# Audio tower on one core: pair 0's norm statistics in two parts, fold copies on ScalarE, pair 0's class row as a matmul, and new queue positions

## What is computed

```
# tok: exponential moving average forward and backward over time, then a linear layer
ewma = (scan(x) + reverse_scan(x)) / 2                  # y[t] = 0.1 x[t] + 0.9 y[t-1]
h    = ewma @ W.T + b                                   # [16, 750, 256]
# attn: two selective scans over time on layernorm(h)
hidden = layernorm(h)
for l in 0, 1:
    delta = softplus(hidden @ Wd[l] + bd[l]);  u = hidden @ Wi[l] + bi[l]
    s     = scan(exp(-delta * softplus(A_log[l])), delta * u)      # state of 64
    hidden = s @ Wo[l] + bo[l] + (s[last] @ Ws[l] + bs[l])         # the class row
h = h + hidden
# ffn on layernorm(h): a shared gated MLP (512 wide) and 16 routed experts (64 wide),
# best 4 of 16 by sigmoid scores, limited to the best 2 of 4 groups of 4
out = h + shared(xn) + sum(w_e * expert_e(xn))
```

## Time and profile before

| | us |
|---|---|
| median of 3 runs (1300.79 to 1304.29) | 1304.12 |
| profiled execution, its own time | 1308.71 |
| its span, first to last instruction | 1306.6 |
| TensorE busy | 1171.1 (90%) |
| VectorE busy | 940.5 (72%) |
| ScalarE busy | 552.0 (42%) |
| GpSimd busy | 414.9 (32%) |

### The profile page before, as it was taken

One profiled execution on the slowest core, in us unless ns is written; L12 is line 12 of the kernel. 1 busy time (PEld: TensorE's weight loads), 2 busy tenths in 40 slices (PEclk: granted clock), 3 DMA queues, 4 the chain that ended last, 5 costly groups with the idle time before them and its releaser, 6 DMA issues.

```text
span 1306.6 us, 24750 instructions
## 1 busy us (share of the span) xinstructions
PE 1171.1 (90%) x7477; PEld 1055.9 (81%) x7477; DVE 940.5 (72%) x2374; ACT 552.0 (42%) x899; POOL 414.9 (32%) x281
## 2 busy tenths in 40 slices
PE   3548886997999989998999889998999999999997
PEld 3437765876998779987988789977998899889997
DVE  6785898598757985889758985799668855644443
ACT  1423552461354533662355434563455343223332
POOL 2022253134131623134321623153402530353233
PEclk8556886998999999999999999999999999999999
DMA  4130021022022413122131323231221321243331
GB/s 125 33 88 17 24 64 42 28 67 75 17 53 42 104 46 57 38 58 70 31 59 30 97 54 54 42 85 33 42 64 28 94 46 36 52 107 62 54 51 19
DMA packets 88288, 71.48 MB, mean 55 GB/s; under 512 B 39671, under 2 KB 82848, under 8 KB 88168
## 3 DMA queue, kind: packets, MB, share of 16 engines
q1 hardware_dynamic: 58832, 43.30, 12.2%
q0 software_dynamic: 26832, 26.06, 11.9%
q10 hardware_dynamic: 2504, 0.55, 0.2%
HBM read 31.36 MB, written 39.34 MB: 54 GB/s over the span
## 4 chain that ended last, share of the span: by engine, by line
PE 65%; DVE 24%; issue 7%; ACT 2%; POOL 1%; another core or an unknown queue 1%; DMA 1%; DVEq 0%; POOLq 0%; ACTq 0%
PE gu_ps L1692 18%; PE gu_ps L1665 14%; PE d_ps L1768 10%; PE d_ps L1749 8%; PE ch_ps L1642 3%; PE ch_ps L1736 3%; DVE h L1188 2%; PE ch_ps L1573 2%; DVE h L1196 2%; DVE stats L1202 1%; PE ch_ps L1728 1%; DVE gu_ps L1453 1%; PE ch_ps L1603 1%; DVE h L1464 1%; PE ch_ps L1591 1%
## 5 line engine op out<-in xcount | busy, mean ns | idle before, releaser
L804 POOL DMA_INDIRECT out_dram<-block_rows,entry x99 | 158.2, 1598 | 316.4 <-ACT block_rows L944 295.7
L1692 PE MATMUL gu_ps<-gu_hi,bx_hi 128*128 x792 | 236.8, 299 | 3.2 <-issue 2.1
L1692 PE MATMUL gu_ps<-gu_lo,bx_hi 128*128 x792 | 225.7, 285 | 0.0
L1692 PE MATMUL gu_ps<-gu_hi,bx_lo 128*128 x792 | 225.7, 285 | 0.0
L932 ACT ACTIVATE hid<-gu_ps 128x512 f32<-128x512 f32 (+1 forms) x195 | 115.0, 592 | 253.9 <-PE gu_ps L1692 120.8
L785 POOL DMA_INDIRECT lists<-records,pos x96 | 135.6, 1412 | 204.1 <-DVE pos L1361 178.3
L1749 PE MATMUL d_ps<-down,hid 128*125 128x256 f32 x768 | 186.0, 386 | 0.0
L1692 PEld LDWEIGHTS gu_ps<-gu_hi,bx_hi 128*128 128x128 f32 x792 | 152.5, 193 | 9.5 <-issue 8.6
L1749 PEld LDWEIGHTS d_ps<-down,hid 128*125 128x125 f32 x768 | 141.5, 192 | 19.5 <-issue 0.3
L1692 PEld LDWEIGHTS gu_ps<-gu_hi,bx_lo 128*128 128x128 f32 x792 | 152.6, 193 | 0.9
L1692 PEld LDWEIGHTS gu_ps<-gu_lo,bx_hi 128*128 128x128 f32 x792 | 151.9, 192 | 0.0
(11 more groups left out here) (279 smaller groups left out, 2866.3 us busy)
## 6 DMA issues: line engine op xcount, KB each, us to landing
block_rows<-lists SPq DMA_DIRECT2D x99, 128.0 KB
out_dram<-h SPq DMA_DIRECT2D x24, 500.0 KB
t<-rstd_scratch SPq DMA_DIRECT2D x21, 250.0 KB, 5.4
x_in<-in_x_dram SPq DMA_DIRECT2D x8, 375.0 KB, 7.5
zt<-in_x_dram SPq DMA_DIRECT2D x7, 375.0 KB
entry<-lists SPq DMA_DIRECT2D x99, 8.0 KB, 3.2
out_dram<-block_rows,entry POOLq DMA_INDIRECT x99
lists<-records,pos POOLq DMA_INDIRECT x96
```

The costliest lines, as they stand in the source:

```text
L804: pool.indirect_dma_start(out=out_rows[0:there, :], out_offset=bass.IndirectOffsetOnAxis(entry[n % UE][:, ID:ID + 1].bitcast(U32), 0), in_ ...
L1692: last = pe.matmul(gu_ps[:, 2 * (g % 2) + half, q * GH:(q + 1) * GH], a[n % 2][:, k, :], w[:, k, bass.ds(of, 1), half * GH:(half + 1) * GH ...
```

## The change

1. Pair 0's `ln1_stats` becomes `ln1_part` 0 (8 of the 12 sub-tiles, after `tok` 3) and `ln1_part` 1 (the last 4), on VectorE and POOL. `rstd_row` 0 and 1 wait for the first part alone, row 2 for both; the rows are taken in the order 0, 1, 2.
2. Copies go from VectorE to ScalarE: `wosT`, `wo_hi`, four of `sbd`, two of `g_hi`, and the high (or only) part of all six `shared` weights. VectorE's differences stay.
3. Pair 0 has no `residual`. Each of its `y` banks gets the class row added by a third matmul for each sub-tile: a stationary operand of ones, 1 x 125, times the row, 1 x 256, in float32. It waits for the class row on TensorE's queue.
4. VectorE's wait for `tokb_bc` moves from behind the tok weights to the first `tok`.
5. Many positions change, for pair 0's preparation and for the steady pairs.

```diff
+        PARTS = (0, 2 * SUB, NJ)
+                elif step == "ln1_part":                       # POOL
+                    j = slice(PARTS[arg], PARTS[arg + 1])
+                    wait(pool, "aggr1", NAGGR * (arg + 1))
+                    inc(pool.tensor_tensor(rstd[0][:, j], mv[0][:, j, 1], mhalf[:, j], ALU.pow), "rstd1")
...
+                elif what == "fold" and n == 1:                # ScalarE
+                    act.wait_ge(S["w_fold"], 16 * W_FOLD)
+                    inc(act.activation(wo_hi[:], wo_raw, ACT.Copy), "wo_hi_done")
+                    act.wait_ge(S["fold_mm"], 4)
+                    inc(act.activation(wosT, ..., ACT.Copy), "wos_ev")
+                elif what == "fold" and n == 2:
+                    act.wait_ge(S["fold_mm"], 5)
...                                                            # 4 copies to sbd, 2 to g_hi
+                elif what == "shared":
+                    act.wait_ge(S["shared_mm"], n + 1)
+                    inc(act.activation(shared_part(n)[0], shared_view(n), ACT.Copy), "shared_hi")
...
-                    dve.wait_ge(S["w_tokb"], 16)               # VectorE, behind tokw 0
+                    wait(dve, "w_tokb", 16)                    # VectorE, in tok
...
-                    wait(pe, "rstd1", 1)                       # rstd_row
+                    wait(pe, "rstd1", sum(SUB * arg >= p for p in PARTS[:-1]))
...
-                                             start=(w is wo_hi), stop=(w is wo_lo))
+                                             start=(w is wo_hi), stop=(w is wo_lo and pair > 0))
+                        if pair == 0:
+                            wait(pe, "row_ev", 1)
+                            last = pe.matmul(bank[0:TP, n * D:(n + 1) * D],
+                                             one[0:1, 0:1].broadcast_to([1, TP]),
+                                             rows[0:1, b, :], start=False, stop=True)
```

More of the change, by code:

```diff
@@ L127 @@
     (1, "list", 11): dict(POOL=21.0),
-    (1, "list", 6): dict(POOL=16.5),
+    (1, "list", 6): dict(POOL=14.5),
     (0, "route_top", 0): dict(DVE=10.5),
@@ L131 @@
     (0, "route_marks", 0): dict(DVE=12.0),
-    (1, "list", 8): dict(POOL=19.5),
-    (1, "table", 0): dict(DVE=14.5),
+    (1, "list", 8): dict(POOL=17.5),
+    (1, "table", 0): dict(DVE=14.0),
     (0, "list", 0): dict(POOL=11.0),
-    (0, "ln1_stats", 0): dict(POOL=-26.5),
     (0, "list", 8): dict(POOL=12.5),
@@ L173 @@
     (1, "score_exp", 0): dict(ACT=5.5),
-    (0, "spread", 0): dict(SP=-19.5),
-    (1, "list", 0): dict(POOL=11.5),
+    (0, "spread", 0): dict(SP=-18.5),
+    (1, "list", 0): dict(POOL=9.5),
     (1, "spread", 0): dict(SP=-26.0),
     (0, "split", (1, 0)): dict(ACT=-6.5, DVE=-8.0),
-    (1, "rstd_row", 1): dict(PE=-23.5),
-    (0, "carry", 0): dict(DVE=-14.0),
+    (0, "carry", 0): dict(DVE=-14.0, PE=-13.5),
     (0, "ewma", 1): dict(SP=-24.0),
@@ L192 @@
     (1, "residual", 5): dict(DVE=-1.5),
+    (0, "split", (0, 0)): dict(ACT=-13.5),
+    (0, "split", (0, 1)): dict(ACT=-13.5),
+    (0, "rstd_t", 0): dict(ACT=-22.0),
+    (2, "residual", 1): dict(DVE=-6.5),
+    (2, "list", 8): dict(POOL=16.0),
+    (0, "residual", 2): dict(DVE=-5.0),
+    (1, "list", 7): dict(POOL=14.5),
+    (2, "list", 0): dict(POOL=12.5),
+    (2, "route_pick", 0): dict(DVE=8.0),
+    (1, "route_pairs", 0): dict(DVE=6.5),
+    (0, "x2t", (2, 1)): dict(ACT=5.0),
+    (0, "score_exp", 0): dict(ACT=5.5),
+    (0, "rstd_row", 2): dict(ACT=-21.0),
+    (0, "ln1_part", 1): dict(POOL=-20.5),
+    (2, "list", 7): dict(POOL=15.5),
+    (0, "tok", 1): dict(DVE=-27.0),
+    (2, "ewma", 1): dict(ACT=-28.0),
+    (2, "split", (0, 0)): dict(ACT=-14.0),
+    (0, "pre", (0, 1)): dict(PE=-19.5),
+    (1, "ln1_part", 1): dict(DVE=-24.0),
+    (1, "route_order", 0): dict(DVE=7.0),
 }
@@ L317, in ticks @@
             for step, arg, at in CHAIN:
-                if q and step == "rstd_row" or q == 0 and step in ("rstd_t", "spread"):
+                if q and step in ("rstd_row", "ln1_part") or q == 0 and step in (
+                        "rstd_t", "spread", "ln1_stats", "residual"):
                     continue
```

234 lines of the change are left out of this document (123 added, 111 removed).

## The result

Measured side by side, the changed kernel took 1290.53 us (median of 4 runs, 1287.21 to 1290.73) and the kernel before 1302.63 (4 runs, 1300.79 to 1304.29): a ratio of 0.9887, 95% interval 0.9864 to 0.991. It is faster by 1.13%, where the forecast (1304.1 to 1296) was 0.6%. The time lies inside the predicted range. Measured again, the ratio was 0.9914 (0.9889 to 0.9939). The profiled execution took 1287.21, span 1285.2, where that of before took 1308.71.

The account below looks back on a forecast made before the run. TensorE was taken to bound the steady pairs, a serial chain through all engines the stretch before the first slot. Terms 5.3 + 2.0 + 0.5 = 7.8 us took the median from 1304.1 to 1296; 80% range 1288 to 1303.

Parts of the forecast that it names:

- Tok bias 0.8: Pair 0's start: the reverse scan no longer waits for the tok bias, so VectorE's work moves 0.8 us earlier.
- Statistics and rows 2.7: Pair 0's preparation: split statistics let the projections start at 33.7, not 36.41; shift 2.7 us, bounds 1 to 4.5.
- Layer 0, 3.9: Pair 0's first scan: starts at 48.4 instead of 52.34; shift 3.9 us, bounds 2.5 and 5.5.
- layer 1, 2.35: Pair 0's second-layer scan: copies and transposes give some back, start 65.0 instead of 67.34; shift 2.35 us.
- Class row and y, 5.7 at the fourth y: Pair 0's y stage: VectorE loses residuals, TensorE gains float32 products; fourth y at 84.6, not 90.28; bounds 4 and 8.
- rival 3: Pair 0's y stage: float32 products queue up on TensorE without overlap, making the kernel slower, 1306 to 1308; chance 8%.
- First slot 5.3: Pair 0 up to its first shared slot: y (2,0) before logit 0 gives back 0.4; shift 5.3, bounds 3.5 and 7.5.
- Ticks 7 to 11, 2.0: Pair 0's later ticks: one of two POOL and VectorE collisions goes, saving 2.0 us; bounds -2 and 5.
- Steady pairs 0.5: Later pairs: residual 0 leaves POOL's ew_lo, last list entries do not move; 0.5 us in all, bounds -3 and 5.
- Rival 2: Stalls that go take clock losses with them: 7.5 at first slot, 5 at tick 10, 1.5 later; 1290; chance 20%.
- Rival 1: TensorE and ScalarE eat half: first slot gains 3, later ticks nothing; 1301; chance 22%.
- Rival 4: Pair 0's statistics split does nothing, since projections do not wait for row 0; counted inside Rival 1, no own chance.

Follow-up runs that it names:

- stats_whole: Changed kernel with pair 0's statistics in one part again (twelve columns in one power, after tok 5): 1299.07 us.
- before_again: The kernel before, unedited, profiled a second time: pairs 2 to 5 took 580.34 us, first slot at 109.78.
- row_residual: Changed kernel with pair 0's class row added by VectorE again, no row matmul: 1286.19 us against the changed kernel's 1293.67; second time 1282.98.
- copies_dve: Changed kernel with the copies of the folded and shared weights on VectorE again: ratio 0.9926.
- the row kernels: Changed kernel with pair 0's class row added by VectorE (1286.19 us), or by TensorE as two float32r products (first slot 106.77).
- steady_old: Changed kernel with pairs 1 to 7 at their old positions: 1304.98 us against 1305.59 for the kernel before.
- steady_only: Kernel before with pairs 1 to 7 at the changed kernel's positions, pair 0 as before: 1293.41 us.
- pool_old: Changed kernel with every position on GpSimd's queue of pairs 1 to 7 as before: 1304.58 us against 1303.38.
- lists_old: Changed kernel with only GpSimd's list entries of pairs 1 to 7 at their old positions: 1299.68 us.
- resid_early: Kernel before with residual 0 of pairs 1 to 7 ahead of split (1,1): pairs as long as before; no total time given.
- resid_late: Changed kernel with residual 0 of pairs 1 to 7 back behind split (1,1): pairs 2 to 5 together 2.4 and 0.1 us longer than in the changed kernel's profiles.
- before: The kernel before the change, unedited: 1302.63 us beside the changed kernel's 1290.53.

## Why the prediction was right in its range and wrong in its terms

The direction was right and the time lay in the range, but that is luck as far as the mechanism goes. The sum of 7.8 us was 7.3 for the first two stages and 0.5 for the steady pairs; measured, the first two are worth nothing that the times show, and the steady pairs are worth 9.5 to 12. The step that failed is the steady pairs' term, put at 0.5 because the moved places on GpSimd's queue were held to be harmless. The prediction's own sign of being wrong, steady pairs that change by more than 1 us each, came: they are 2.1 to 3.1 us shorter.

- **Tok bias 0.8.** Right: the reverse scan is at 6.94, 0.90 earlier.
- **Statistics and rows 2.7.** The step failed in size: L1651's first product is at 30.83, 5.6 earlier, not at 33.7. The first row came at 24.57 (forecast 24.3), but I took rows at 1.82 and fold 2 at 2.08 from low-clock rows. They took 1.05 to 1.13 and 1.16. That TensorE had idled 6.27 ahead of the old rows was in the same group of rows; I had named the case ("if the rows ran at the higher level") and put it outside the sum. The six small copies took 0.91 + 0.55 = 1.46; I took 1.2. The Trainium skill's rule of "ScalarE: Activation LUTs", section What ACT_TABLE_LOAD costs, had given 1.1, so the measurement is a third above it. `stats_whole` prices the split at 7.7 at the first scan.
- **Layer 0, 3.9; layer 1, 2.35.** They were to stand 3.9 and 2.35 earlier, and were 7.5 and 6.9 earlier than in the old trace, the same error carried on. Against `before_again` they are 5.3 and 4.7, as the old trace itself ran with a low clock in 24 to 48 us (0.54, where that one had 0.76).
- **Class row and y, 5.7 at the fourth y.** The stage was to gain 3.35 and gained nothing (22.9 us both). The term that failed is the float32 product: 0.86 estimated by doubling, measured 1.14 from its start to the next load of weights (67.65 to 68.79), and the two products between two of them take 0.72 (68.79 to 69.51), not 0.43. So a y is 2 x 1.86 = 3.72. This is rival 3's mechanism, and `row_residual` shows it: 5 us at the first slot, 0.4 to 0.6% in the time.
- **First slot 5.3.** From the old to the new trace it is 4.4. But five kernels with the old pair 0 reach it at 109.53 to 111.63 and eight with the changed one at 107.19 to 109.71 (`copies_dve`, `stats_whole` and the row kernels left out); the medians, 109.78 and 108.5, are 1.3 apart.
- **Ticks 7 to 11, 2.0.** The placing wait of 4.66 is gone as forecast, but the collisions were miscounted: one was to stay. The routed subtractions now meet a `route_t` (2.38 at 138.83), a split and, with two of them in a row, another `route_t`, and TensorE's wait for `hid` grew:

```profile
150.20 2.68 DVE L1221 TENSOR_TENSOR states<-t,states 64x750 fp32r<-64x750 f32 x1
...
166.19 4.71 POOL L785 TENSOR_TENSOR dr_lo<-dr_lo,dr_hi 128x1024 fp32r<-128x1024 f32 x2
...
166.68 4.25 DVE L1458 TENSOR_SCALAR route_t<-upto 1x6 f32<-1x6 f32 x1
...
175.92 0.78 PE L1718 MATMUL gu_ps<-x_hi,up_hi 128*128 128x500 f32 x1 [6.49 <-DVE hid L1491]
```

  This last `route_t` takes 4.24 or 4.25 us in all thirteen kernels with the new preparation, and 1.94 or 1.95 in all five with the old: `routed` 4 and 5 stand together at tick 11.4, where before only `routed` 5 stood. The prediction had this case as its lower bound (-2, all three later parts collide again), and by the lock a saving of 0 or below. TensorE's waits from 112 to 232 us, before and then changed:

```profile
PE gu_ps L1665 <- DVE hid L1444: 4.8, 2, 4.6
PE ch_ps L1649 <- DVE route_t L1308: 4.7, 1, 4.7
```

```profile
PE gu_ps L1718 <- DVE hid L1491: 9.7, 2, 6.5
PE ch_ps L1621 <- DVE h L1243: 7.6, 2, 6.8
```

  Pair 1 starts at 221.64, and in the old trace at 228.69, but at 222.84, 221.95, 222.73 and 223.82 in the four other kernels with the old pair 0; of the eight with the changed one the median is 223.0. The profiled execution that the sum rests on reached pair 1 some 6 us later than these. So the first two stages together, 7.3 in the sum, are worth about 0; `steady_old`, ratio 0.9996 (0.9969 to 1.0022), says the same within 4 us. They hold two large effects of opposite sign, the split's gain and the row products' loss.
- **Steady pairs 0.5.** The step that failed worst. They are worth 577.97 - 568.52 = 9.5 us in pairs 2 to 5, and by `steady_only` 12 in the time. Two sentences were wrong. "The last list entries do not move" looked at the last two and not at the ten others, which help to set when `fw` and `ew_lo` run; `pool_old` and `lists_old` show that GpSimd's positions carry the gain. "`residual 0` leaves POOL's `ew_lo`" was right, and worth nothing: by `resid_early` and `resid_late` its place does not matter. The reason given, that TensorE's waits behind such steps are under 1 us a pair, was read from waits alone. Over pairs 2 to 5 TensorE's whole idle time fell by 5.5 us, and its busy time for the same number of records by 4.0, which no table of waits shows.
- **Rivals.** Rival 2's 1290 was met in number and not in mechanism. Rival 1 describes the first two stages best (y paced at the low clock, nothing from the later ticks), but not the time. Rival 3 held inside its stage. Rival 4 fell by `stats_whole`.

## What to carry to other kernels

Where two engines lock each other out, the other engine's start time counts, so count every entry ahead of the locked operation in its queue: here 1 us on GpSimd's queue decided which VectorE instruction was stretched. Look in a steady stretch for instructions of one form with two durations (0.68 and 2.27 here). They show where to try a new order, but not what it is worth: `resid_late` has three residuals stretched by 1.2 to 1.8 us each and is only 0.1 to 2.4 us longer over the four pairs. An operation moved to an engine with idle time is free only if that idle time lies in the same stretch; in the y stage TensorE was paced by the product it had been given. When you price waits, compare the busy time of the same instructions too: here it made up 4.0 of 9.45 us. And a sum made on one profiled execution inherits its clock: a second profile of the same kernel moved pair 1's start by 6 us, nearly as much as the change was to bring.

## What the runs showed of the hardware

- Executions of the same kernel differ by the clock that pair 0 gets. The old kernel in 24 to 48 us:

```profile
24.00:48.00 24.00, 14.79 (x58) 12.81 (x58) 12.01 (x38) 9.15 (x12) 2.31 (x1) 0.54 0.03 8
```

```profile
24.00:48.00 24.00, 10.66 (x58) 9.35 (x58) 13.84 (x44) 9.55 (x11) 2.31 (x1) 0.76 0.03 7
```

  The same 58 products took 14.79 us at 0.54 and 10.66 at 0.76. Of 22 runs of the old kernel, measured together, the times went from 1300.5 to 1314.2 us and the mean clocks from 0.949 to 0.938.
- At the lower level a float32 product of one row by 256 columns took 1.14 us from its start to the next load of weights, which waited 0.65 of them; the pair of float32r products that replaces it took 0.71, and the next load waited 0.23.
- A power of 4 columns took 1.01 us, of 8 columns 1.68 and of 12 columns 2.31 (`before`) and 2.49 (`stats_whole`): split in two it costs 0.2 to 0.4 more.
- A VectorE instruction can be held although its record starts first: `pool_old`'s split begins 0.33 us before `fw` and takes 2.95, `lists_old`'s `table` begins 0.8 us before `fw` and takes 2.62. A scalar operation on 1 x 6 elements took 4.25 us beside two GpSimd subtractions of 4.71 together.
